# Adding the two states of a pair by accumulating DMAs instead of by GpSimd's additions

## The reference, cut to what matters

```python
A = -jnp.exp(A_log)                      # (1024, 16)
def step(h, inp):
    dt_t, B_t, C_t, u_t = inp            # (2,1024) (2,16) (2,16) (2,1024)
    dA = jnp.exp(dt_t[:, :, None] * A)
    h = h * dA + (dt_t * u_t)[:, :, None] * B_t[:, None, :]
    y = jnp.einsum('bdn,bn->bd', h, C_t) # sum over the 16 states
    return (h, y)
h0 = jnp.zeros((b, DI, N), xn.dtype)
_, ys = jax.lax.scan(step, h0, seq)
y = jnp.transpose(ys, (1, 0, 2)) + u * D_param
y = y * jax.nn.silu(z)
```

## Time and profile before

| what | value |
|---|---|
| time, two runs | 2406.16 and 2406.65 us, median 2406.4 |
| span of the profiled execution | 2405.4 us (1.0 below the median; its own time is not given apart) |
| VectorE busy | 2163.1 us, 90% of the span |
| GpSimd busy | 1908.1 us, 79% |
| TensorE busy | 2232.3 us, 93% |
| ScalarE busy | 1679.7 us, 70% |
| GpSimd's additions L1407 | 133, 169.0 us |
| GpSimd's products L1402 | 512, 1199.2 us |
| the scan | from about 75 to 1921 us of the span |
| the DMA engines | 21.6% of the time of sixteen, all issued by SyncE |

### The profile page before, as it was taken

The page is one execution under the profiler, slowest core; times in us unless marked ns, Lnnn a source line. Parts: engine busy times, 40 slices in busy tenths (PEclk is TensorE's granted clock), DMA queues, the critical chain, the costliest instruction groups (busy, mean ns, idle before and its releaser), DMA issues. The chain is left out here.

```text
span 2405.4 us, 24262 instructions
## 1 busy us (share of the span) xinstructions
PE 2232.3 (93%) x6966; PEld 1153.2 (48%) x6966; DVE 2163.1 (90%) x2363; ACT 1679.7 (70%) x3268; POOL 1908.1 (79%) x1244
## 2 busy tenths in 40 slices
PE   9899999989998999899989988998987999999999
PEld 3233434334433443344334333433333488988888
DVE  4899999999999999999999999999999966666666
ACT  3688777877787778778877887787555445466655
POOL 0699999999999999999999999999987822232225
PEclk9899999999999999999999999999998999999999
DMA  6610231041104110411051123103100121011113
GB/s 225 229 44 27 100 103 40 27 148 59 35 27 158 47 37 22 167 56 59 19 179 40 31 71 130 33 27 130 64 31 12 74 77 34 26 56 58 49 53 123
DMA packets 78050, 176.10 MB, mean 73 GB/s; under 512 B 7453, under 2 KB 10781, under 8 KB 77918
## 3 DMA queue, kind: packets, MB, share of 16 engines
q1 hardware_dynamic: 77918, 174.56, 21.6%
HBM read 157.23 MB, written 17.30 MB: 73 GB/s over the span
## 5 line engine op out<-in xcount | busy, mean ns | idle before, releaser
L1402 POOL TENSOR_TENSOR arena<-arena 128x1024 f32<-128x1024 f32 x512 | 1199.2, 2360 | 107.1 <-ACT arena L580 77.3
L1001 DVE TENSOR_TENSOR_SCAN arena<-ps,arena 128x512 f32<-128x512 f32 x1024 | 1241.7, 1256 | 1.3 <-ACT ps L580 1.2
L580 ACT ACTIVATE ps<-arena 128x512 f32<-128x512 f32 x1087 | 722.8, 681 | 367.2 <-DVE arena L1001 307.0
L318 PE MATMUL ps<-arena,keep 128*128 128x512 f32 x1782 | 863.3, 615 | 108.2 <-POOL arena L1402 74.9
L989 DVE TENSOR_TENSOR arena<-ps,arena 128x1024 f32<-128x1024 f32 x512 | 618.4, 1208 | 13.8 <-PE ps L318 11.1
L318 PEld LDWEIGHTS ps<-arena,keep 128*128 128x128 f32 x1782 | 333.6, 194 | 592.2 <-issue 338.4
L264 PE MATMUL ps<-arena 128*128 128x512 f32 x1024 | 459.9, 593 | 1.6 <-issue 0.8
L264 PEld LDWEIGHTS ps<-arena 128*128 128x128 f32 x1024 | 193.5, 190 | 248.8 <-issue 247.8
L580 ACT ACTIVATE arena<-arena 128x2 f32<-128x2 f32 (+2 forms) x599 | 228.4, 384 | 52.1 <-POOL arena L1347 17.1
L304 PE MATMUL ps<-arena 128*128 128x512 f32 x512 | 231.1, 592 | 0.0
L1359 POOL TENSOR_TENSOR arena<-arena 128x512 f32<-128x512 f32 x168 | 213.9, 1273 | 10.9 <-ACT arena L580 3.8
(11 more groups left out here) (146 smaller groups left out, 2701.7 us busy)
## 6 DMA issues: line engine op xcount, KB each, us to landing
arena<-scr_bc SPq DMA_DIRECT2D x128, 512.0 KB, 6.4
arena<-in_inT SPq DMA_DIRECT2D x128, 256.0 KB, 2.6
arena<-in_x SPq DMA_DIRECT2D x17, 512.0 KB, 4.3
scr_x<-arena SPq DMA_DIRECT2D x32, 256.0 KB, 2.2
arena_b<-scr_x SPq DMA_DIRECT2D x16, 512.0 KB, 3.8
arena_c<-scr_x SPq DMA_DIRECT2D x32, 256.0 KB, 2.9
out<-arena_c SPq DMA_DIRECT2D x32, 256.0 KB, 2.0
arena<-in_x SPq DMA_DIRECT2D x30, 256.0 KB, 3.3
```

Source lines behind the costliest of these rows:

```text
L318: last = e.matmul(YP, ident, hb[G % R][:, i, :], start=False, stop=(g == NG - 1 and i == n - 1))
L580: return e.activation(o_, i_, f, **kw)
L1001: e.tensor_tensor_scan(H, DA[s % 4], H, h0, MUL, ADD).then_inc(v_sc)
L1402: m_ = e.tensor_tensor(H, H, Ct[:, GN * g:GN * g + GN, :], MUL)
```

## The change

The product by C now tells `g_w` itself, for every pair. For a halved pair GpSimd then waits for that product and issues a DMA that adds the second state to the first within SBUF (source `H[:, 1, :]`, destination `H[:, 0, :]`, 128 rows of 2 KB, `accum_op=ADD`), on a semaphore of the buffer (`d_hs`). TensorE waits for that semaphore besides `g_w` before it takes the single matmul of a halved pair; `hs_no` counts how often a buffer has been halved so far. The semaphores of the last layer's `o_bufs` transfers are now those of the B and C loads, which are over by then, with their count as an offset (`D0`). The set of halved pairs, the tables and every other instruction are as they were.

```diff
-        d_xo = [sem(f"d_xo{i}") for i in range(4)]
-        d_out = [sem(f"d_out{i}") for i in range(4)]
+        d_xo, d_out, D0 = d_B[0:4], d_C[0:4], 16 * NCH
+        d_hs = [sem(f"d_hs{i}") for i in range(R)]
...
+        hs_no = {}
+        for G in range(NG * NU):
+            if halved(*divmod(G, NG)):
+                hs_no[G] = 1 + sum(H % R == G % R for H in hs_no)
...
                 e.wait_ge(g_w, G + 1)
+                if G in hs_no:
+                    e.wait_ge(d_hs[G % R], 16 * hs_no[G])
                 n = 1 if halved(U, g) else GN
...
-                    m_ = e.tensor_tensor(H, H, Ct[:, GN * g:GN * g + GN, :], MUL)
+                    e.tensor_tensor(H, H, Ct[:, GN * g:GN * g + GN, :], MUL).then_inc(g_w)
                     if halved(U, g):
-                        halves += 1
-                        m_.then_inc(g_m)
-                        e.wait_ge(g_m, halves)
-                        m_ = e.tensor_tensor(H[:, 0, :], H[:, 0, :], H[:, 1, :], ADD)
-                    m_.then_inc(g_w)
+                        e.wait_ge(g_w, G + 1)
+                        e.dma_start(H[:, 0, :], H[:, 1, :], accum_op=ADD).then_inc(d_hs[G % R], 16)
...
-                    e.wait_ge(d_xo[i], 16 * (K // 2 + 1))
+                    e.wait_ge(d_xo[i], D0 + 16 * (K // 2 + 1))
...
-                        e.wait_ge(d_out[i], 16 * (K // 2))
+                        e.wait_ge(d_out[i], D0 + 16 * (K // 2))
```

More of the change, by code:

```diff
@@ L144, in program @@
                                     "att", "y", "o"))
-        g_c, g_r1, g_r2, g_r3, g_rs, g_nm, g_tap, g_dt, g_du, g_gw, g_m, g_w = (sem("g_" + n) for n in ("c", "r1", "r2", "r3", "rs", "nm", "tap", "dt", "du", "gw", "m", "w"))
+        g_c, g_r1, g_r2, g_r3, g_rs, g_nm, g_tap, g_dt, g_du, g_gw, g_w = (sem("g_" + n) for n in ("c", "r1", "r2", "r3", "rs", "nm", "tap", "dt", "du", "gw", "w"))
         g_att, g_m1, g_mask, g_l1, g_l2, g_lrs, g_q, g_xo = (sem("g_" + n) for n in ("att", "m1", "mask", "l1", "l2", "lrs", "q", "xo"))
@@ L1378, in _ @@
             rs(1)
-            halves = 0
             for s in range(NS):
@@ L1666, in _ @@
             for i in range(4):
-                e.wait_ge(d_out[i], 16 * 8)
+                e.wait_ge(d_out[i], D0 + 16 * 8)
 PACK = [("c", 16), ("A_log", 128), ("ada_b", 8), ("ln_g", 4), ("ln_b", 4), ("conv_w", 32), ("conv_b", 8),
```

## The result

| | before | after |
|---|---|---|
| time, two runs each, median | 2406.4 us | 2484.43 us (2484.14 and 2484.73) |
| span of the profiled execution | 2405.4 us | 2482.9 us |
| mean granted clock over the span | 0.984 | 0.965 |

After stands to before as 1.0323, with a 95% interval from 1.0293 to 1.0353: slower by 78 us. The forecast was 2422.

The account below looks back on a forecast made before the run. VectorE (98.7% busy) and GpSimd (97.5%) were taken to share the limit. Latency of 3.5 us in tile 6, 11.5 in tile 7 and 0.8 at the end made 16 on the 2405.4 span; median 1.0 above: 2422, range 2398 to 2490.

Parts of the forecast that it names:

- the cost of 0 for tiles 0 to 3: 96 of 133 pairs: TensorE comes 5.6 us after the addition in tile 1, hiding 3.0 us of latency; cost 0.
- dear issue: Rival in GpSimd's queue: above 1.6 us per issue GpSimd sets the pace; 2474 at 2.0 us, 2522 at 2.36; chance 0.22.
- I take 1.27: GpSimd's 133 DMA issues each take 1.27 us, like the addition, so GpSimd is loaded as before.
- 3.0 on quiet DMA engines: Landing assumed for a 256 KB adding transfer away from loads: 3.0 us, between copies of 2.2 and 3.3.
- 5.7 for pairs 3 to 5 of tile 7 and 4.0 for pair 7: Landings assumed on loaded DMA engines; margins subtracted, tile 7 costs 2.3 us, times 5 = 11.5 us.
- ScalarE's exponentials of the next unit come from dt some steps ahead: Behind a late sum ScalarE waits for VectorE often enough to follow, so VectorE is who waits in the end.
- that only pulls upward: Granted clock of 0.79 after TensorE's wait; longer waits might make tile 0's sums later; left out of the sum.
- Tile 6, pair 5 … 3.5 us: Margin of 2.5 us against a 3.0 us landing: cost 0.5 us, 7 times, 3.5 us.
- The end: After the last product the pair is ready at 1921.0, delaying TensorE's last sum and y_fin; cost 0.8 us.
- The gain: Rival: GpSimd's freed time removes VectorE's waits, 22 us over the scan, giving 2385; chance 0.02.
- the rule: An add in the DMA path reads two sources, so 1.0 us more per landing; sum some 31 us instead of 16.

Follow-up runs that it names:

- e1: Changed kernel with adding DMAs only in tiles 7 and 0 (61 of 133 pairs), GpSimd's additions for the other halved pairs; 2485.57 us.
- e2: Changed kernel with adding DMAs only in tiles 1, 2, 3 and 6 (72 pairs), GpSimd's additions in tiles 7 and 0; 2428.21 us.
- e3: Changed kernel with the B and C loads of chunks 1 to 7 cut to a quarter of their columns; 2465.46 us.
- e8: Changed kernel with each adding DMA cut to 64 of the 512 columns, the rest left out of the sum; 2458.28 us.
- e9: Changed kernel with the same DMAs as plain copies of all columns, without the add; 2454.21 us.
- e11: Changed kernel with DMAs for only 28 pairs whose sums TensorE takes late, GpSimd's addition for the other 105; 2411.22 us.
- e12: Changed kernel with pairs 0 and 5 of tile 7 (12 of the 133) added by GpSimd again; 2496.42 us.
- e14: Changed kernel with DMAs in tiles 0, 1, 2, 3 and 6 (103 pairs), GpSimd's additions in tile 7; 2443.0 us.
- e15: Changed kernel with DMAs in tile 7 alone (30 pairs), GpSimd's additions everywhere else; 2457.78 us.
- e16: Changed kernel with B and C loads of chunks 1 to 7 a quarter as wide and each adding DMA a plain copy of 64 of 512 columns; 2433.97 us.
- e17: Kernel with DMAs everywhere but tile 7, plus three filling matmuls before TensorE's wait for pair 5 of tile 0 from the second chunk on; 2436.43 us.
- e4: Changed kernel with neither addition nor DMA, the second state of the 133 halved pairs left out of the sum; 2397.9 us.

## Why the prediction was wrong

The mechanism was right: issues that cost GpSimd no more than the additions, the latency as the price, and TensorE's waits for DMAs that reach VectorE through its buffers and y_fin. Its size was not, 75 us in the scan against 16. Two steps failed: the cost of 0 for tiles 0 to 3, and the landings beside other transfers. The loss lies where the prediction said that it would be wrong, in tiles 0 to 2 (58.5 of 75.4 us). That 2484 lies inside its range, which ends at 2490, is luck: the upper end stood for a dear issue, and there was none.

**The margins, read for every pair.** How much do the margins themselves explain? An estimate from the rows of before: each of the 133 sums becomes ready later by 0.30 + landing - 1.35 us. TensorE keeps its order and catches up only in its idle gaps. An expand or y_fin waits if its sum isn't done, and all that follows VectorE's wait moves with it. ScalarE, GpSimd's own queue and the clock are left out. With the landings that each run's trace shows, us lost in the scan:

| run | estimate | measured |
|---|---|---|
| after | 80 | 75.4 |
| e1, tiles 7 and 0 | 65 | 75.1 |
| e2, tiles 1, 2, 3, 6 | 29 | 21.5 |
| e3, thin loads | 60 | 56.1 |
| e8, small adds | 56 | 51.1 |
| e9, plain copies | 50 | 48.0 |
| e11, 28 pairs | 4 | 4.9 |
| e12, two pairs back | 61 | 86.9 |
| e14, not tile 7 | 41 | 34.6 |
| e15, tile 7 alone | 38 | 49.6 |
| e16, thin and small | 31 | 27.7 |

So the margins of the undisturbed trace give about the whole loss, once every pair is taken and its delay is followed down TensorE's queue. With the forecast's own latencies (3.0 us later, 5.7 and 4.0 in tile 7) the same estimate gives 60 us: 39 from tiles 0 to 3, 3.5 from tile 6, 17 from tile 7. With 3.4 us for every landing of after it gives 31: the 40 landings that took at least 1 us more than that carry more than half. With 1.8 for every landing of e16 it gives 4, so most of e16's last 27 us are its long landings.

Step by step:

- **"I take 1.27" for the issue.** It held, partly by luck: the price is made of parts that the forecast didn't have. The row is 0.89 us, with 0.30 of wait ahead; the next product starts 0.27 before the row's end and takes 2.66 instead of 2.35 (781.44 after the issue of 780.82; medians 2.65 and 2.36). 0.30 + 0.89 - 0.27 + 0.31 = 1.23 us of GpSimd, where the addition with its wait took 1.27 + 8.4 / 107 = 1.35. The dear issue is refuted: GpSimd is busy for 1312 of the 1440 us, where it would have had to be full.
- **"3.0 on quiet DMA engines".** 3.4, but counted from the start of the issue: the forecast added a whole issue ahead of the landing. Ready 0.30 + 3.4 = 3.7 us after the product in place of 1.35, 2.35 later, less than the 3.0 that I put in.
- **"5.7 for pairs 3 to 5 of tile 7 and 4.0 for pair 7".** In the five chunks pair 3 took 5.1 to 5.6 and pair 4 3.3; pair 5 took 5.7 to 9.2 and pair 7 4.1 to 7.8. I took the landing of one load for a whole tile. With after's landings the estimate for tile 7 alone is 37 us in place of 17.
- **Pair 0 of tile 7** was not in the sum. It falls into the first batch of loads (seven from 744.25 on in before), and its addition ended at 747.59, 0.4 us ahead of TensorE's sum at 748.02. It lands after 8.4 to 9.0 us, makes the longest wait, 7.30 us, and VectorE's 3.65.
- **"Tiles 0 to 3 … Cost 0"** failed, and it is the largest error. It rests on one pair, and e11 shows that pair to be free. I took it for 96. Pair 5 of tile 0 had 1.2 us. In e14, where tile 7 is out of it, these tiles lose 33 us against the forecast's 0, and by its own 3.0 us it should have been 39. "3.0 on quiet DMA engines" doesn't hold for all of them either: 5.1 to 5.3 us at pair 5 of tile 0 in units 8 to 24.
- **"ScalarE's exponentials of the next unit come from dt some steps ahead"**: ScalarE couldn't follow at a boundary, it waits 3.34 and 5.06 us there, and the first reaches GpSimd (5.02) and so the next issue. The estimate leaves this out. In e15 it is 12 us short and in e12 26, runs whose loss lies in tiles 7 and 0, so the handing-on may be worth that much there; no run parts it from the rest.
- **The clock** was left out as a side effect "that only pulls upward". Half clock stood for 3.2 of the 5.2 us at tile 0's y_fin in e14, and for 7 us in that kernel's time (e17).
- **"Tile 6, pair 5 … 3.5 us"**: none measured (-0.7 in after). **The end**: 0.8 us forecast, 0.2 measured between the last scan and y_fin. **The gain**: 10 us were there at most (e4), and none came.

Where I cited the Trainium skill, "Collectives: The Full Stack", on an add that reads two sources: e9 has the number, 3.4 with the add and 2.4 without, the 1.0 us that I worked out by the rule. That the two agree is partly luck, since 0.30 of it is the longer issue and only 0.7 the transfer. By the rule my sum would have been some 31 as I put it (28.8 by its own terms), still less than half of the loss. The box of "SBUF — State Buffer" in the Trainium skill on VectorE locking the port for GpSimd's descriptors: all 133 issues took 0.867 to 1.097 us with VectorE busy beside them, so nothing locked them, as by the page's own condition.

Why does a landing take 9 us? The packets of the DMA engines tell how, though not why. In the 4.4 us after pair 0's issue at 770.10 the engines carry SyncE's queue alone (770 to 774.5 us). The packets of GpSimd's queue start at 774.9 and share the engines with the loads until 778.7 (774.5 to 779.2 us):

```profile
q1 hardware_dynamic: 332, 1.22, 95.6%
...
q0 software_dynamic: 144, 0.26, 30.3%
```

A quiet adding DMA starts 1.5 us after its issue and moves for 1.5; this one starts after 4.8 and moves for 3.9.

What stays open: why the first packet waits 3.3 us longer beside loads; which of the pairs of tile 7 a schedule of the loads could protect (no run moved the loads); and what ScalarE's and GpSimd's lateness adds in e12 and e15.

## What to carry to other kernels

Moving a small operation from an engine into a DMA trades busy time for latency. Before counting it as hidden, list for every moved instance (not for one of a kind) how long the consumer's in-order queue is behind it, and what loads are in flight there. Then follow each delay down that queue to the next buffer or result that somebody needs. Here one pair read for 96 gave 0 us, and all of them with the same latency 39. And ask first what the freed engine is worth; a run that leaves the operation out (10 us here) puts the ceiling on the whole idea.

## What the runs showed of the hardware

- An accumulating DMA within SBUF of 128 rows of 2 KB lands 3.3 us after the start of its issue at the quickest and 3.4 in the median, a plain copy after 2.4 (e9), an accumulating one of 128 rows of 256 bytes after 2.2 (e8), and a plain one of that size after 1.8 (e16; medians). An eighth of the bytes saves a third of the add's landing and a quarter of the copy's.
- GpSimd's issue of an accumulating DMA is a row of 0.886 us, of a plain one 0.587, at either size (after, e8; e9, e16).
- Issued when five 512 KB loads had gone out in the 2.2 us before it and two followed, it lands after 9 us, 3.3 of them because its first packet starts later than on quiet engines. With the loads' bytes cut to a quarter the longest landing was still 7.7 (e3).
- GpSimd's first product after a DMA issue takes 0.3 us longer (2.65 against 2.36, medians of 84 and 436), and the issue's own row overlaps it by 0.27.
- After a wait of 3.10 us of TensorE the granted clock was 0.50 for the next 4 us (816 to 820 of e14), and two rows of a sum took 2.05 us in place of 1.12. With the wait filled the clock was 1.00 in the same work (813 to 817 of e17):

```profile
816.00:820.00 4.00, 4.00 (x5) 1.43 (x5) 4.00 (x4) 3.52 (x8) 4.00 (x3) 0.50 0.45 116
```

```profile
813.00:817.00 4.00, 4.00 (x11) 1.81 (x10) 4.00 (x4) 3.17 (x7) 4.00 (x3) 1.00 0.30 77
```
